# Feed-forward hidden columns: the 42 that five chunks leave over, packed into one tile

## The reference

```
x = x + local_attention(shift(x)) @ wo          # window 128, 8 heads of 64
h = shift_token(x)                              # half of the columns from the token before
h = layernorm(h) * lg + lb
h = h @ w1 + b1                                 # 256 -> 2 * HID, HID = 682
a, g = jnp.split(h, 2, axis=-1)
h = a * jax.nn.gelu(g, approximate=False)
x = x + h @ w2 + b2                             # 682 -> 256
```

## Time and profile before

| | us |
|---|---|
| median of 3 runs | 2305.5 (2302.86 to 2305.98) |
| the profiled execution: its time | 2307.47 |
| its span (first to last instruction) | 2305.7 |
| PE busy in the span | 2019.4 (88%) |
| DVE busy | 1440.5 (62%) |
| ACT busy | 1109.5 (48%) |
| POOL busy | 1098.9 (48%) |
| mean granted TensorE clock | 0.948 of full |

### The profile page before, as it was taken

How to read it: one execution, slowest core, us unless ns; L and a number is a source line. 1 busy time by engine, 2 the same in 40 slices (tenths; PEclk the granted TensorE clock), 3 DMA queues, 4 the chain that set the end, 5 groups by cost and what they waited for, 6 DMA issues and landing times. The chain is left out here.

```text
span 2305.7 us, 43659 instructions
## 1 busy us (share of the span) xinstructions
PE 2019.4 (88%) x13824; PEld 1417.0 (61%) x13888; DVE 1440.5 (62%) x2744; ACT 1109.5 (48%) x2339; POOL 1098.9 (48%) x903
## 2 busy tenths in 40 slices
PE   6869999999977989989987999689999899699986
PEld 5623433433425777777765888567677677478875
DVE  5658877778825777777765443366776776554424
ACT  3406655656654556566554222255655655432213
POOL 3431121212216655655643878456556556187840
PEclk9859999999988999999997999799999999799988
DMA  6893545655411000000012111200000002111137
GB/s 210 261 181 45 77 64 71 84 70 74 69 33 36 23 17 23 23 17 23 23 55 56 55 55 37 72 18 23 17 23 23 17 23 64 46 41 55 46 95 238
DMA packets 163937, 143.24 MB, mean 62 GB/s; under 512 B 30326, under 2 KB 144350, under 8 KB 163678
## 3 DMA queue, kind: packets, MB, share of 16 engines
q1 hardware_dynamic: 162462, 140.23, 25.9%
q10 hardware_dynamic: 1344, 1.31, 0.2%
HBM read 90.89 MB, written 50.35 MB: 61 GB/s over the span
## 5 line engine op out<-in xcount | busy, mean ns | idle before, releaser
L650 DVE TENSOR_REDUCE ca_mx<-ca_pR 128x1 f32<-128x512 f32 (+3 forms) x768 | 375.6, 549 | 89.0 <-PE ca_pR L520 46.5
L627 ACT ACTIVATE ca_pr<-ca_pS 128x1024 f32<-128x1024 f32 (+3 forms) x384 | 300.3, 814 | 242.0 <-PE ca_pS L544 183.9
L879 ACT ACTIVATE w_pe<-w_pS,w_nmax 128x256 f32<-128x256 f32 x512 | 236.6, 487 | 223.7 <-DVE w_nmax L989 223.7
L802 POOL TENSOR_TENSOR w_tsn<-w_qk,w_tab 128x512 f32<-128x512 f32 x128 | 168.8, 1340 | 344.9 <-DVE w_pn L998 333.8
L459 POOL TENSOR_SCALAR_AFFINE_SELECT ca_pr<-ca_pr 128x256 f32<-128x256 f32 x256 | 103.9, 406 | 428.4 <-ACT ca_pr L627 426.1
L517 PE MATMUL ca_pR<-ca_ks,ca_qs 96*128 96x512 bf16 (+3 forms) x768 | 240.1, 349 | 19.7 <-DVEq L703 17.0
L810 POOL TENSOR_TENSOR w_rs<-w_ssc,mhalf 128x16 f32<-128x16 f32 x64 | 250.9, 3920 | 5.3
L1105 PE MATMUL w_pX<-w_pt,w_v 128*64 128x128 f32 x2048 | 173.0, 290 | 76.5 <-DVE w_pt L1003 41.7
L544 PE MATMUL ca_pS<-ca_qs,ca_ks 98*128 98x512 bf16 (+3 forms) x768 | 190.5, 331 | 14.6 <-issue 12.8
L1105 PEld LDWEIGHTS w_pX<-w_pt,w_v 128*64 128x64 f32 x2048 | 111.3, 139 | 128.0 <-DVE w_pt L1003 66.3
L517 PEld LDWEIGHTS ca_pR<-ca_ks,ca_qs 96*128 96x128 bf16 x768 | 73.1, 98 | 187.3 <-DVE ca_mx L650 126.7
(11 more groups left out here) (163 smaller groups left out, 4699.5 us busy)
## 6 DMA issues: line engine op xcount, KB each, us to landing
QKP<-p_parts SPq DMA_DIRECT2D x32, 384.0 KB, 3.4
ca_qs<-QKP SPq DMA_DIRECT2D x96, 128.0 KB, 6.6
ca_ks<-QKP SPq DMA_DIRECT2D x96, 128.0 KB, 7.1
VA<-p_vaug SPq DMA_DIRECT2D x8, 1024.0 KB, 5.4
ca_va<-VA SPq DMA_DIRECT2D x16, 512.0 KB, 10.5
w_xt<-X SPq DMA_DIRECT2D x64, 128.0 KB, 2.0
X<-w_x SPq DMA_DIRECT2D x64, 128.0 KB, 1.7
f_hh<-X SPq DMA_DIRECT2D x32, 256.0 KB, 5.0
```

The source lines that it names most:

```text
L627: act.activation(pr[:, k % 2, pair, :, 0:w], pS[:, pair, :, 0:w], ACT.Exp, scale=CS).then_inc(p_ready, 1)
L650: dve.tensor_reduce(mx[:, i, h, ch:ch + 1], pR[jb % RING][:, 0:w], AX.X, ALU.max, negate=True).then_inc(ring_free, 1)
L802: pool.tensor_tensor(dst, src[:, :, ::-1, :], s, ALU.mult).then_inc(S["ts_ready"], 1)
L879: ins = act.activation(pe_[:, h], pS[:, bank, slot], ACT.Exp, bias=nmax[:, n:n + 1], accum_out=sums[:, h:h + 1])
```

## The change

The names `WHOLE = 5` (full chunks), `TAIL = 42`, `GATE_ROW = 64` and `TAIL_COL = 1280` are new. The weight tile now has the 5 x 128 value columns, the 5 x 128 gate columns, and then one tile of 128 columns that holds the 42 last value columns at 0 to 41 and the 42 last gate columns at 64 to 105. The last chunk of up is one group of 6 matmuls into `pH[:, 1, 1]`, value rows on partitions 0 to 41 and gate rows on 64 to 105. The gelu of that chunk works on partitions 64 to 105. gated of that chunk is two instructions over 42 partitions, one that writes af's rows 0 to 41 and one that writes rows 64 to 105, with the same values. POOL rounds the whole tile into ahi, and makes no alo for that chunk; a new DVE step, `tail_low`, overwrites ahi's rows 64 to 105 with the low part. w2's last chunk holds its 42 rows twice, at 0 and at 64, so that two matmuls (by w2's high and low part) take in the high and low part of the activations together; down has 17 matmuls for a token tile instead of 18. tail_low(s) stands on DVE inside residual(s-1), ahead of the last of its four additions, and for superstep 0 at the end of the part ahead of the loop, in front of lo_of(2).

w1 comes by four DMAs instead of two, the biases by four (three before), w2 by three (two before); the biases are issued ahead of the wait for the cleared tiles, and b1g is no longer cleared. w1's high and low parts are made in three parts (1536, 1024 and 256 elements for each partition) instead of two (1536 each).

```diff
             def start_feed():
-                HA = HC * P
+                HA = WHOLE * P
                 sp.wait_ge(S["w_split"], ONE + 4 * layer + 4)
...
-                for half, n in ((0, HA), (1, HID)):
-                    sp.dma_start(qkv_st[:, :, half * HA:half * HA + n],
-                                 w1[layer][:, half * HID:half * HID + n].rearrange("(k p) n -> p k n", p=P))\
-                      .then_inc(F.sems["w1_loaded"], 16)
+                for half in range(2):
+                    for to, first, n in ((half * HA, half * HID, HA),
+                                         (TAIL_COL + half * GATE_ROW, half * HID + HA, TAIL)):
+                        sp.dma_start(qkv_st[:, :, to:to + n],
+                                     w1[layer][:, first:first + n].rearrange("(k p) n -> p k n", p=P))\
+                          .then_inc(F.sems["w1_loaded"], 16)
...
-            pool.memset(qkv_st[:, :, HC * P + HID:2 * HC * P], 0.0).then_inc(F.sems["cleared"], 1)
+            pool.memset(qkv_st[:, :, TAIL_COL:TAIL_COL + P], 0.0).then_inc(F.sems["cleared"], 1)
...
-            load(b1a[:, :], b1[layer][0:HA].rearrange("(c p) -> p c", p=P), True)
-            sp.wait_ge(S["cleared"], ONE + 3 * layer + 3)
-            load(w2_st[:, 0:HC - 1], w2[layer][0:(HC - 1) * P].rearrange("(c p) n -> p c n", p=P))
-            load(w2_st[0:TAIL, HC - 1], w2[layer][(HC - 1) * P:HID])
...
+            for half, bias in ((0, b1a), (1, b1g)):
+                first = half * HID
+                load(bias[:, 0:WHOLE], b1[layer][first:first + HA].rearrange("(c p) -> p c", p=P), True)
+                load(bias[GATE_ROW:GATE_ROW + TAIL, WHOLE:HC],
+                     b1[layer][first + HA:first + HID].rearrange("(p c) -> p c", c=1), True)
+            sp.wait_ge(S["cleared"], ONE + 2 * layer + 2)
+            load(w2_st[:, 0:WHOLE], w2[layer][0:HA].rearrange("(c p) n -> p c n", p=P))
+            for row0 in (0, GATE_ROW):
+                load(w2_st[row0:row0 + TAIL, WHOLE], w2[layer][HA:HID])
...
 # POOL, split
-                pool.wait_ge(S["a_hi"], ONE + u + 1)
-                pool.tensor_tensor(alo[:, j, ch], af[:, ch % 2], ahi[:, j, ch].bitcast(F32), ALU.subtract)\
-                    .then_inc(S["a_lo"], 1)
+                if ch < WHOLE:
+                    pool.wait_ge(S["a_hi"], ONE + u + 1)
+                    pool.tensor_tensor(alo[:, j, ch], af[:, ch % 2], ahi[:, j, ch].bitcast(F32), ALU.subtract)\
+                        .then_inc(S["a_lo"], 1)
...
 # DVE, gated
+                else:
+                    rows = slice(GATE_ROW, GATE_ROW + TAIL)
+                    for row0 in (0, GATE_ROW):
+                        ins = dve.scalar_tensor_tensor(af[row0:row0 + TAIL, ch % 2], pH[0:TAIL, ch % 2, 1],
+                                                       b1a[rows, ch:ch + 1], gl[rows, ch % 2], ALU.add, ALU.mult)
+                    ins.then_inc(S["act_ready"], 1)
+
+            def tail_low(s, j):
+                u = (g0 + s) * HC + WHOLE
+                rows = slice(GATE_ROW, GATE_ROW + TAIL)
+                dve.wait_ge(S["a_hi"], ONE + u + 1)
+                dve.tensor_tensor(ahi[rows, j, WHOLE], af[rows, WHOLE % 2], ahi[rows, j, WHOLE].bitcast(F32),
+                                  ALU.subtract).then_inc(S["a_lo"], 1)
...
 # DVE, residual
                 for n in range(SUP):
+                    if n == SUP - 1 and within(s, 1) is not None:
+                        tail_low(s + 1, 1 - j)
                     dve.wait_ge(S["o_ready"], ONE + (g0 + s) * SUP + n + 1)
...
 # PE, up
-                    for half in range(2):
-                        cols = slice(half * HA + ch * P, half * HA + (ch + 1) * P)
+                    for half in range(2) if ch < WHOLE else (1,):
+                        col = half * HA + ch * P if ch < WHOLE else TAIL_COL
+                        cols = slice(col, col + P)
...
 # PE, down
-                    terms = [(t, m, ch) for ch in range(HC) for t, m in ((ahi, w2_hi), (ahi, w2_lo), (alo, w2_hi))]
+                    terms = [(t, m, ch) for ch in range(WHOLE) for t, m in ((ahi, w2_hi), (ahi, w2_lo), (alo, w2_hi))]
+                    terms += [(ahi, w2_hi, WHOLE), (ahi, w2_lo, WHOLE)]
```

More of the change, by code:

```diff
@@ L51 @@
 NEG = -1e30
+WHOLE = HID // P
+TAIL = HID - WHOLE * P
+GATE_ROW = 64
+TAIL_COL = 2 * WHOLE * P
 ONE = 1
@@ L1238, in chunks_of @@
     def chunks_of(w, part):
-        half = slice(part * HA // 2, (part + 1) * HA // 2)
-        return w[:, :, :].rearrange("p k (z c) -> p k z c", z=2)[:, :, :, half]
+        if part == 2:
+            return w[:, :, TAIL_COL:TAIL_COL + P]
+        half = slice(3 * P * part, (3, WHOLE)[part] * P)
+        return w[:, :, 0:TAIL_COL].rearrange("p k (z c) -> p k z c", z=2)[:, :, :, half]
     with nc.Block() as block:
@@ L1255, in _ @@
             load(b2t[:, :], b2[layer][None, :].broadcast_to([P, D]))
-            load(b1a[:, :], b1[layer][0:HA].rearrange("(c p) -> p c", p=P), True)
-            sp.wait_ge(S["cleared"], ONE + 3 * layer + 3)
-            load(w2_st[:, 0:HC - 1], w2[layer][0:(HC - 1) * P].rearrange("(c p) n -> p c n", p=P))
-            load(w2_st[0:TAIL, HC - 1], w2[layer][(HC - 1) * P:HID])
-            load(b1g[:, 0:HC - 1], b1[layer][HID:HID + (HC - 1) * P].rearrange("(c p) -> p c", p=P), True)
-            load(b1g[0:TAIL, HC - 1:HC], b1[layer][HID + (HC - 1) * P:2 * HID].rearrange("(p c) -> p c", c=1), True)
+            for half, bias in ((0, b1a), (1, b1g)):
[4 more added lines that the diff above has]
+            sp.wait_ge(S["cleared"], ONE + 2 * layer + 2)
+            sp.sem_inc(K.passed, 1)
+            load(w2_st[:, 0:WHOLE], w2[layer][0:HA].rearrange("(c p) n -> p c n", p=P))
+            for row0 in (0, GATE_ROW):
+                load(w2_st[row0:row0 + TAIL, WHOLE], w2[layer][HA:HID])
             def load_x(s, j):
@@ L1342, in _ @@
         def _(act):
-            act.wait_ge(S["w1_loaded"], ONE + (layer + 1) * 2 * 16)
-            act.wait_ge(S["cleared"], ONE + 3 * layer + 3)
-            for part in range(2):
+            act.wait_ge(S["w1_loaded"], ONE + (layer + 1) * 4 * 16)
+            for part in range(3):
                 act.activation(chunks_of(w1_hi, part), chunks_of(w1_st, part), ACT.Copy).then_inc(S["w_hi"], 1)
@@ L1363, in gelus @@
                     act.wait_ge(S["act_ready"], ONE + u + 1)
-                    act.activation(gl[:, ch % 2], pH[:, ch % 2, 1], ACT.Gelu, bias=b1g[:, ch:ch + 1])\
+                    rows = slice(0, P) if ch < WHOLE else slice(GATE_ROW, GATE_ROW + TAIL)
+                    act.activation(gl[rows, ch % 2], pH[rows, ch % 2, 1], ACT.Gelu, bias=b1g[rows, ch:ch + 1])\
                        .then_inc(S["gelu_done"], 1)
@@ L1368, in _ @@
             turned(0, 0)
-            act.wait_ge(S["w_loaded"], ONE + (layer + 1) * 6 * 16)
+            act.wait_ge(S["w_loaded"], ONE + (layer + 1) * 8 * 16)
             act.activation(w2_hi[:, :, :], w2_st[:, :, :], ACT.Copy).then_inc(S["w_hi"], 1)
@@ L1428, in _ @@
             normalise(0, 0, 0)
-            for part in range(2):
-                dve.wait_ge(S["w_hi"], ONE + 3 * layer + part + 1)
+            for part in range(3):
+                dve.wait_ge(S["w_hi"], ONE + 4 * layer + part + 1)
                 dve.tensor_tensor(chunks_of(w1_lo, part), chunks_of(w1_st, part), chunks_of(w1_hi, part).bitcast(F32),
@@ L1438, in _ @@
             gated(0, 0, 1)
-            dve.wait_ge(S["w_hi"], ONE + 3 * layer + 3)
+            dve.wait_ge(S["w_hi"], ONE + 4 * layer + 4)
             dve.tensor_tensor(w2_lo[:, :, :], w2_st[:, :, :], w2_hi[:, :, :].bitcast(F32), ALU.subtract)\
@@ L1448, in _ @@
                     normalise(2, 0, 1)
+            tail_low(0, 0)
             def step(s, j, it):
@@ L1495, in _ @@
             turn(0, 0)
-            pe.wait_ge(S["w_split"], ONE + 3 * layer + 1)
+            pe.wait_ge(S["w_split"], ONE + 4 * layer + 1)
             def midway():
-                pe.wait_ge(S["w_split"], ONE + 3 * layer + 2)
+                pe.wait_ge(S["w_split"], ONE + 4 * layer + 3)
                 turn(1, 1)
             up(0, 0, midway)
-            pe.wait_ge(S["w_split"], ONE + 3 * layer + 3)
+            pe.wait_ge(S["w_split"], ONE + 4 * layer + 4)
             pe.sem_inc(K.passed, 1)
```

14 lines of the change are left out of this document (8 added, 6 removed).

## The result

The changed kernel is slower by 0.4%: 2316.97 us (median of 10 runs, 2310.57 to 2323.49) against 2307.72 us (10 runs, 2302.86 to 2312.8) for the kernel before, ratio 1.0041, 95% interval 1.0027 to 1.0056. That is about 9 us. The forecast was 2300.0 with a range of 2288 to 2309.

A forecast was written before the change was run, and what follows sets the result against it. The prediction took TensorE to bound the feed-forward steps, with no idle time. Its terms, -8.4 (steps 6 and 7), -1.0 (starts), +0.8 (steps 2 to 5), +3.1 (clock), made -5.5 us from 2305.5: 2300.0, range 2288 to 2309.

The forecast's parts named there:

- The edge on the third tile: Way down, steps 2 to 5: TensorE's third tile waits 1.87 us for VectorE's first residual addition; +0.8 us in all.
- the saving only in steps 6 and 7: Steps without moments, plus the last way down, keep the saving: 4.2 us a layer, -8.4 in both.
- the 24.3 that was named as a sign: Sign that the forecast is right: GpSimd's step takes 24.3 us in step 6, 26.1 to 26.3 in steps 2 to 5.
- the rule that was weighed: VectorE instruction starting in another partition quarter is held until earlier ones finish; 1.4 us more, 2301.4; left out of the sum.
- The layer's start: Superstep 0 onward: GpSimd bounds the stretch and gets relief, -0.5 us a layer, -1.0 in both, bounds -1.3 and +2.2 each.
- the new stall of 1.6 us: Layer 1's start: TensorE waits for gated of chunk 0, queued behind tail_low and tlo; taken as hidden by GpSimd's stretch.
- eight such waits: Third-tile waits of 1.87 us, in steps 2 to 5 of each layer, where a later superstep's moments are computed.
- The clock: TensorE's granted clock may fall after idle times of about 1.7 us; two falls taken, +3.1 us.
- The bound of 12.4: Upper end of the clock's price for eight third-tile waits, between 0 and 12.4 us.
- The sum: All terms: -8.4 - 1.0 + 0.8 + 3.1 = -5.5 us, giving 2300.0.
- Rival C: Slower: clock falls at every new third-tile wait and twice at the layers' starts; +6.9 us, 2312.4; chance 0.13.
- Rival B: TensorE keeps all or most of the saving: 27 us, 2278; half of it 2290; chance 0.15.

The follow-up runs named there:

- e9: Changed kernel with GpSimd's addition of b2 for superstep s-1 moved behind the split of chunk 0 of superstep s: 2323.34 us, ratio 1.0056 to before.
- e2: Changed kernel with tail_low moved behind gated of chunk 0 of the next superstep, with its own semaphore: 2311.7 us, ratio 1.0009 to before.
- e6: Changed kernel with a third multiplication of the same form ahead of the last chunk's two, into a tile nothing reads: 2319.87 us, ratio 1.0046 to before.
- e14: Changed kernel with each superstep's 8 transposes issued twice, same values into the same tile: 2318.88 us, one run.
- e3: Changed kernel with first residual addition ahead of gated of chunk 5 and tail_low behind the next superstep's gated of chunk 0: 2283.95 us, ratio 0.9886.
- e13: e3 with superstep 2's normalise ahead of superstep 1's tlo at the layer's start: 2281.18 us, ratio 0.9882 to before.
- e1: Changed kernel with the first residual addition of superstep s-1 moved ahead of gated of chunk 5 on VectorE: 2291.45 us, ratio 0.9914 to before.
- e12: The kernel of e6 traced once more, unchanged: 2319.57 us, one run.

## Why the prediction was wrong

**The edge on the third tile: right.** It forecast a wait from 19.47 to 21.34 us of the step, steps of 26.2 to 26.25 us in steps 2 to 5, and the saving only in steps 6 and 7. Measured: waits of 1.89 to 1.91 us idle (1.7 forecast), 26.30 and 26.46 us where the clock stayed, and -4.2 us a layer at the end, as forecast. Step 6 took 23.48 us, 1.89 less than its 25.37 before; the 24.3 that was named as a sign overlooked that this step has no transposes. Most of the missing 0.2 us of idle time are those of the rule that was weighed: from gated's start to the addition's it is 1317.29 to 1318.82, 1.53 us, not 0.66 + 0.67 = 1.33, and the two multiplications start 0.76 apart. The rule that an instruction in another quarter of the partitions is held (the Trainium skill, VectorE: DVE Perf Modes, section on two Vector instructions with no wait between them) gave 1.51; the trace agrees, and I should have put it into the sum.

**The layer's start: this step failed.** I forecast -0.5 us for each layer; measured +3.75 and +5.50. Three parts of it were wrong. I had the stretching on the wrong engine: the earlier trace rows show GpSimd's rounding stretched beside a VectorE subtraction, and I charged the 1.0 to 1.5 us to GpSimd's addition; here VectorE's was the later one to start and it was the one that stretched, 0.69 to 2.85, in the queue that TensorE waits for. The Trainium skill, SBUF — State Buffer, section SBUF: two separate sides, has the rule that I left out: the two engines share a pair of ports as a lock, and, where VectorE's instruction has two SBUF inputs and GpSimd's reads SBUF, whichever starts first keeps it to its end. The trace agrees for this pair: tail_low ended 0.55 us after the addition (1268.11 + 2.37 = 1270.48, 1271.03). Behind a rounding it doesn't hold in full: here VectorE's tlo started 0.14 us behind GpSimd's rounding and took 1.55 us instead of 1.23, so it can't have stood still until the rounding's end.

```profile
1258.06 1.50 POOL L1326 TENSOR_SCALAR f_ahi<-f_af 128x512 fp32r<-128x512 f32 x1
1258.20 1.55 DVE L1415 TENSOR_TENSOR f_tlo<-f_hf,f_thi 128x1024 fp32r<-128x1024 f32 x1
```

e9 shows that the stretch of tail_low comes from the addition of b2 beside it, and e2 what its place in the queue is worth (3.1 and 4.4 us). Second, I took the new stall of 1.6 us for one that GpSimd hides and gave it no fall of the clock; it was 3.52 us, and the clock fell behind it in both layers (about 2.1 us each). Third, superstep 1 computes moments as well and has the same wait on the third tile, 1.90 us and a fall; I counted eight such waits and there are ten.

**The clock: mis-sized.** I took two falls in steps 2 to 5, 3.1 us; there were four, 4 x 1.53 = 6.1 us, and two more in superstep 1, which are in the starts. The bound of 12.4 held, but the picture behind it, that a length between 1.51 and 2.10 us is the question, is refuted by e6 and e14: 2.57 us and even 3.54 had no fall behind them in some places, and 1.9 us had one in some and none in others.

**The sum.** -8.4 at the end as forecast; steps 2 to 5 +8.2 instead of +3.9 (0.8 + 3.1); the starts +9.25 instead of -1.0: 9.0 instead of -5.5. Rival C named this outcome, +6.9 us by falls behind the new waits and at the starts, and got 0.13; that many falls weren't needed, since the starts cost the rest. Rival B is refuted as the change stands (and half of its 27 us would have been 2292, not 2290), but e3 and e13 show that 24 to 27 us are there: one addition moved ahead of one instruction on VectorE frees 25 us of what the changed kernel takes (e1), and a later tail_low the rest.

## What to carry to other kernels

Before taking work from the engine that bounds a loop, list what its later instructions wait for and how much room each wait has: here the room was 0.5 us and the saving 1.9, so the loop stayed as long and an idle gap came in. Look in the queue of the engine that releases them for an instruction that could go first, since the time for it is already idle there. And price idle gaps in a matmul stream twice, once by their length and once by the clock that may fall behind them; read the second price as a range, since here equal gaps fell or didn't.

## What the runs showed of the hardware

- Where VectorE subtracts one SBUF tile from another beside a GpSimd instruction that reads SBUF, the later to start is stretched, whichever engine it is: tail_low 0.07 us behind GpSimd's addition took 2.85 us instead of 0.69, while GpSimd's rounding 0.16 us behind VectorE's tlo took 2.47 instead of 1.48 (tlo started at 2042.54). How much depends on what stands in front: behind a GpSimd rounding of 1.50 us, 0.14 us after its start, tlo took 1.55 us instead of 1.23.
- The same idle time of 1.90 us had a fall of the granted clock behind it in 4 of 8 steps in each of two traces of the changed kernel and in none of the 8 steps of 27.3 us in e14; idle times of 2.57 us had fewer (3 of 10 in each of two traces) than 1.90 (6 of 10 in each of two), and of 1.14 us none. A wait of 3.5 us at a layer's start had a fall behind it in both layers of the changed kernel and in only one of the two layers in e6 and in e12.
- A fall cost TensorE 1.4 to 1.6 us on the way down, and twice 2.8 to 2.9 us (e6, e9).
- A VectorE instruction over 42 partitions takes what one over 128 takes (0.75 us for 512 elements), and two in a row from partitions 0 and 64 start 0.76 us apart, not 0.66.
